# Moving the tiny per-token columns of two layer norms into an idle PSUM bank of a four-layer transformer kernel

## The chip, the cores and the metric

The kernel runs on one core of one Trainium2 chip. The metric is the device time of one execution in microseconds (us); lower is better. The engines are TensorE (PE in the profile), VectorE (DVE), ScalarE (ACT), GpSimd (POOL) and SyncE (SP, which here only issues DMAs). Each has its own instruction queue, works in order, and waits for the others through semaphores.

## What is computed

The input `x` has 2 x 512 tokens of 1024 features, the context has 2 x 1024 tokens. Four residual blocks follow each other, each behind a layer norm without weights:

```
x = x + tanh(g_xattn[0]) * fake_quant(LN(x)) @ fake_quant(ctx)
x = x + tanh(g_ffn[0])   * (quant_per_token(LN(x)) @ dequant(W_int).T + bias)
x = x + tanh(g_xattn[1]) * attention(LN(x), ctx, ctx; Wq, Wk, Wv, Wo)
x = x + tanh(g_ffn[1])   * (LN(x) @ dequant_fp4(packed).T)

LN(x)              = (x - mean(x)) / sqrt(var(x) + 1e-5)
quant_per_token(x) = clip(round(x / s), -127, 127) * s,  s = clip(max|x|, 1e-8) / 127
```

The change concerns the second norm (with the per-token quantisation behind it) and the third norm. Both need, for each token, a handful of single numbers: the mean, the variance, its inverse root, the quantisation step.

## The kernel before

The 1024 tokens lie on 128 partitions in T = 8 tiles `t`; `X[:, t, :]` (128 x 1024, fp32, in SBUF) is the residual stream of tile `t`. A per-token number of all tiles is a column block of 8: `mv[:, t, 0:2]` (mean, variance), `sd` (the square root that ScalarE makes), `rr` (inverse root), `ra` (a scratch), `am` (absolute maximum), `step_`, `ninv` (minus one over the step), `sB` (scale of the second product), `bb` (bias of the third norm), `nhalf`. All of them lie in SBUF, all in fp32.

The stages: up to about 150 us the context and the weights are prepared, the first norm is made and K and V are projected. Then comes the stage that the change touches, called the AB stage here (about 151 to 252 us): product "a" (first residual block) and product "b" (second) of the 8 tiles, in the order of the list `AB_OPS` (L165): a0 to a4, b0, a5, b1, a6, b2, a7, b3 to b7. TensorE's `stage_ab` (L1462) fills three pairs of PSUM banks in turn, banks (0,1), (4,5), (2,3) (`AB`, L164); it may begin operation i only when VectorE has emptied operation i - 3 (L1477). Banks 6 and 7 (`sbank` 2 and 3) are not used by it: their last use before it is the transposes of the integer weights (`wd_turn`, L1386, emptied by `wd_high` and `wd_low`), and bank 7's next use is the attention (`sum_half`, L1559).

VectorE's order in the AB stage is written out by hand in L1195 to L1229. For each tile it does

- `a_out(t)` (through `ab_out`, L1137): X = product * scale + X for the two halves, two SCALAR_TENSOR_TENSOR of 128x512 at L1146; then `a_stats(t)` (`stats`, L1003): mean and variance;
- `ln2_reduce(t)` (L1160): the maximum over |mean - x| that ScalarE has written (`ln2_deviation`, L767), then three tiny operations to the step and to `ninv`, for which ScalarE's `ln2_round` (L772) waits;
- `ln2_clip(t)` (L1170): the clip of the 16-bit quantised tile at L1172, after which SP transposes it by DMA for product b;
- `ln2_scales(p)` (L1174), once for tiles 0 to 3 and once for 4 to 7: the inverse root by `root_of` (L1010, one Newton step on the reciprocal of ScalarE's square root) and `sB`; `b_out` needs `sB`;
- `b_out(t)` (L1156): the same as `a_out` for product b with `sB` as scale, and the statistics of the third norm;
- `ln3_affine(p)` (L1180) for each pair of tiles: `root_of` again and `bb`; ScalarE's `y3_out` (L784) waits for it and makes the normalised tile and its 16-bit high part, GpSimd's `y3_low` (L515) the low part, and SP transposes both.

`d()` is an explicit drain, so each tiny operation starts after the one before it has written. The first norm's `ln1_affine` (L1050) uses `root_of` too and isn't touched.

GpSimd's order is also written by hand (L519 to L544): `wq_low(k)` (a TENSOR_SCALAR at L504 and a TENSOR_TENSOR at L506, 128x1024), `add_bias(t)` (TENSOR_TENSOR, L513), `add_c2(t)` (L493), `y3_low(t)` (L517). ScalarE has its own (L810 to L835): deviation, rounding, the square roots (`ln_sd`, L673), `wq_high(k)` (L797) and `y3_out(t)`. SP issues `xt2`, `next_wq`, `xt3` in L352 to L362, then the load `praw` of the packed weights (L365), the stores of q (`store_q`) with `xt3(6)` and `xt3(7)` between them (L394 to L397).

Behind the AB stage: the q projection (`q_proj`, from 245 us), with the unpacking of the last weights on VectorE (`unpack`, L1236, which begins only when all of `xt3` has landed, L1279), then from 325 us the score maxima, the attention and the last two products.

Of the kernel before, what the change touches and what calls it, by code (L numbers as in the profile page):

```python
# [21 lines left out]
ALU = mybir.AluOpType  # L22
AX = mybir.AxisListType
# [5 lines left out]
EPS = 1e-5  # L29
MAGIC = 12582912.0  # L30
ZC = 128.0
WS = 256.0
# [5 lines left out]
def build(nc, x, ctxt, g_xattn, g_ffn, x1s, x1z, x2s, x2z, W_int, scale_i32, bias, Wq, Wk, Wv, Wo,  # L38
# [4 lines left out]
    T = B * S // P  # L43
    TB = S // P
# [31 lines left out]
    with ExitStack() as ctx:  # L76
        def sb(name, shape, dt):
            return ctx.enter_context(nc.sbuf_tensor(name, shape, dt))

        def sem(name):  # L80
            return ctx.enter_context(nc.semaphore(name))
# [3 lines left out]
        bank = [mpair[0][:, 0, :], mpair[0][:, 1, :], mpair[1][:, 0, :], mpair[1][:, 1, :],  # L85
                sbank[0][:, :], sbank[1][:, :], sbank[2][:, :], sbank[3][:, :]]
# [23 lines left out]
        mv = sb("mv", [P, T, 2], F32)  # L110
        rs = sb("rs", [P, 8], F32)
        sd = sb("sd", [P, T], F32)
        nhalf = sb("nhalf", [P, T], F32)
        rr = sb("rr", [P, T], F32)
        bb = sb("bb", [P, T], F32)
        ra = sb("ra", [P, T], F32)
        sB = sb("sB", [P, T], F32)
        am = sb("am", [P, T], F32)
        step_ = sb("step", [P, T], F32)
        ninv = sb("ninv", [P, T], F32)  # L120
# [20 lines left out]
        at = [0, SET, 8192]  # L141
# [12 lines left out]
        dev = [cx[:, 2 + i, :] for i in range(2)]  # L154
# [10 lines left out]
        AB_OPS = ([("a", t) for t in range(5)] + [("b", 0), ("a", 5), ("b", 1), ("a", 6), ("b", 2), ("a", 7)]  # L165
                  + [("b", t) for t in range(3, T)])

        acc_sb = y[:, 0:512]
        rsum_sb = y[:, 512:1024]
        sumT_sb = vtmp[:, 0:512]  # L170
# [27 lines left out]
        s = {n: sem(n) for n in names}  # L198
# [721 lines left out]
        def _(dve):  # L920
            v = nc.vector

            def d():

                dve.drain()  # L925
# [9 lines left out]
            def consts():  # L935
                dve.wait_ge(s["gates_ok"], 1)
                v.reciprocal(IS1, S1)
                v.reciprocal(IS2, S2)
                v.tensor_tensor(AL, TX0, S1, ALU.mult)
                v.tensor_scalar(NZ1, Z1, -1.0, ZC, ALU.mult, ALU.add)  # L940
                v.tensor_scalar(NZ2, Z2, -1.0, ZC, ALU.mult, ALU.add)
                v.tensor_scalar(BE, TF0, 1.0 / WS, None, ALU.mult)
                v.tensor_scalar(GA, TX1, 1.0 / WS, None, ALU.mult)
                v.tensor_scalar(NBE, TF0, -1.0 / WS, None, ALU.mult)
                d()
                v.tensor_tensor(AL, AL, S2, ALU.mult)
                v.tensor_tensor(KZZ, NZ1, NZ2, ALU.mult)
                d()
                v.tensor_tensor(NZ1A, NZ1, AL, ALU.mult)
                v.tensor_tensor(NZ2A, NZ2, AL, ALU.mult)  # L950
                v.tensor_tensor(KZZ, KZZ, AL, ALU.mult)
                d()
                v.tensor_scalar(KZZ, KZZ, float(D), None, ALU.mult).then_inc(s["consts_ok"], 1)
# [56 lines left out]
            def root_of(first, n, ok, at):  # L1010

                c = slice(first, first + n)
                v.tensor_scalar(nhalf[:, c], mv[:, c, 1], EPS, -0.5, ALU.add, ALU.mult)
                dve.wait_ge(ok, at)
                v.reciprocal(rr[:, c], sd[:, c])
                d()
                v.tensor_tensor(ra[:, c], rr[:, c], rr[:, c], ALU.mult)
                d()
                v.tensor_tensor(ra[:, c], ra[:, c], nhalf[:, c], ALU.mult)
                d()  # L1020
                v.scalar_tensor_tensor(out=rr[:, c], in0=ra[:, c], scalar=1.5, in1=rr[:, c], op0=ALU.add, op1=ALU.mult)
                d()
# [46 lines left out]

            turned_low(0, 0)  # L1070
            consts()
            wkv_low(2)
            turned_low(1, 2)
# [46 lines left out]
            c = NCH - 1  # L1120
# [38 lines left out]

            def ln2_reduce(t):  # L1160
                dve.wait_ge(s["ln2_dev"], t + 1)
                v.tensor_reduce(am[:, t:t + 1], dev[t % 2], AX.X, ALU.max, apply_absolute_value=True)
                d()
                v.tensor_scalar(step_[:, t:t + 1], am[:, t:t + 1], 1e-8 * EPS ** 0.5, 1.0 / 127.0, ALU.max, ALU.mult)
                d()
                v.tensor_scalar(ra[:, t:t + 1], step_[:, t:t + 1], -1.0, None, ALU.mult)
                d()
                v.reciprocal(ninv[:, t:t + 1], ra[:, t:t + 1]).then_inc(s["ln2_inv"], 1)

            def ln2_clip(t):  # L1170
                dve.wait_ge(s["ln2_q"], t + 1)
# [1 line left out]

            def ln2_scales(p):  # L1174
                c = slice(TB * p, TB * p + TB)
                root_of(TB * p, TB, s["ln2_sd"], p + 1)
                v.scalar_tensor_tensor(out=sB[:, c], in0=step_[:, c], scalar=BE, in1=rr[:, c], op0=ALU.mult, op1=ALU.mult)
                d()

            def ln3_affine(p):  # L1180
                c = slice(2 * p, 2 * p + 2)
                d()
                root_of(2 * p, 2, s["ln3_sd"], p + 1)
                v.scalar_tensor_tensor(out=bb[:, c], in0=mv[:, c, 0], scalar=-1.0, in1=rr[:, c], op0=ALU.mult,
                                       op1=ALU.mult).then_inc(s["ln3_aff"], 1)

            def ln4(t, first=False):
# [8 lines left out]
            a_stats(0)  # L1196
            a_out(1)
            ln2_reduce(0)
            a_stats(1)
            for t in range(2, 5):  # L1200
                a_out(t)
                ln2_clip(t - 2)
                ln2_reduce(t - 1)
                a_stats(t)
                if t == 2:
                    bias_scale()
            ln2_scales(0)
            ln2_clip(3)
            ln2_reduce(4)
            for t in range(5, T):  # L1210
                b_out(t - 5)
                if t == 6:
                    ln3_affine(0)
                a_out(t)
                a_stats(t)
                ln2_clip(t - 1)
                ln2_reduce(t)
            ln2_scales(1)
            b_out(3)
            ln2_clip(7)  # L1220
            ln3_affine(1)
            b_out(4)
            b_out(5)
            ln3_affine(2)
            b_out(6)
            b_out(7)
# [463 lines left out]
```

## Time and profile before

| | us |
|---|---|
| median of 3 runs | 934.3 (928.06, 934.3, 934.41) |
| the profiled execution | 933.91 |
| its span | 932.1 |

| engine | busy, us | share of the span |
|---|---|---|
| PE | 848.9 | 91% |
| DVE | 598.2 | 64% |
| POOL | 534.8 | 57% |
| ACT | 447.6 | 48% |

The span is what the profiler sees from the first to the last instruction of that one execution; 1.8 us of the device time lie around it. The shares are averages over stages with different limits. In the rows below, times are in us from the start of the span, the second number of a timeline row is the time of the instruction (or of the merged group), and brackets give the idle time of the engine before it and what ended it. An instruction that is held up inside its engine shows as a long one, not as idle time before it.

### The profile page before, as it was taken

The numbers are of one execution on the slowest core, as the hardware profiler recorded it, in microseconds if no ns is written. First come the engines' busy times: TensorE is split into PE (matmuls) and PEld (weight loads), VectorE is DVE, ScalarE is ACT, GpSimd is POOL, SyncE is SP. The second block draws the span as 40 slices with busy tenths as digits, with TensorE's granted clock in tenths as the row PEclk, the third lists the DMA queues.
The fourth block names the chain that finished last, engine by engine and source line by source line (L and its number), as shares of the span: only waits on it lengthen the run. The fifth ranks groups of instructions, "written<-read, shape, count | busy, mean of one in ns | idle before, by whom it ended". The sixth has DMA issues, their size and how long they took to land.

```text
span 932.1 us, 14107 instructions
## 1 busy us (share of the span) xinstructions
PE 848.9 (91%) x4456; PEld 333.4 (36%) x4456; DVE 598.2 (64%) x846; ACT 447.6 (48%) x741; POOL 534.8 (57%) x235
## 2 busy tenths in 40 slices
PE   3789899969978797999999999999999998999998
PEld 2656564424433242222222222222222222444443
DVE  3666655988746645777777777877777850264621
ACT  4243425636511112667767767677767776022100
POOL 3544216964732310788888888888888888222100
PEclk9999999989989897999999999999999999999999
DMA  6898873422887421254455444544555334222232
GB/s 203 220 225 228 200 194 91 102 68 63 154 213 201 113 76 54 46 123 99 100 122 122 95 91 104 121 104 93 121 121 113 65 80 91 46 46 56 56 124 79
DMA packets 121673, 107.80 MB, mean 116 GB/s; under 512 B 86176, under 2 KB 106656, under 8 KB 117536
## 3 DMA queue, kind: packets, MB, share of 16 engines
q1 hardware_dynamic: 116160, 73.69, 31.0%
q0 software_dynamic: 4608, 33.56, 17.8%
q8 instruction: 26, 0.43, 0.2%
q10 hardware_dynamic: 864, 0.00, 0.0%
q14 instruction: 15, 0.12, 0.0%
HBM read 41.55 MB, written 12.58 MB: 58 GB/s over the span
## 4 chain that ended last, share of the span: by engine, by line
PE 57%; DVE 16%; issue 9%; DVEq 6%; DMA 6%; SPq 2%; ACT 2%; POOLq 2%; POOL 1%; ACTq 0%
PE sbank L1546 11%; PE sbank L1555 10%; PE mpair L1500 9%; DVEq L925 6%; DVE mx L1262 5%; PE sbank L1632 3%; PE sbank L1647 3%; PE sbank L1634 3%; PE sbank L1649 3%; PE sbank L1636 3%; PE sbank L1399 2%; PE sbank L1401 2%; PE sbank L1400 2%; PE sbank L1565 2%; POOLq L485 2%
## 5 line engine op out<-in xcount | busy, mean ns | idle before, releaser
L1262 DVE TENSOR_REDUCE mx<-mpair 128x1 f32<-128x1024 f32 x256 | 301.1, 1215 | 80.9 <-PE mpair L1500 80.7
L867 ACT ACTIVATE regC<-sbank 128x512 f32<-128x512 f32 x512 | 279.6, 595 | 130.7 <-PE sbank L1546 130.1
L1546 PE MATMUL sbank<-regD 98*128 98x512 f16 x512 | 179.8, 388 | 9.4 <-DMA regD<-mT 5.2
L1500 PE MATMUL mpair<-regD 96*128 96x512 f16 x512 | 158.1, 386 | 11.5 <-DVE mx L1262 6.4
L588 POOL TENSOR_TENSOR wraw<-regC 128x2048 f32<-128x2048 f32 x32 | 145.3, 4541 | 23.4 <-ACT regC L867 14.1
L1555 PE MATMUL sbank<-regC,regD 128*32 128x512 f32 x1024 | 137.2, 608 | 1.0 <-ACT regC L867 1.0
L1546 PEld LDWEIGHTS sbank<-regD 98*128 98x128 f16 x512 | 46.6, 97 | 202.1 <-ACT regC L867 162.3
L588 POOL TENSOR_TENSOR regD<-regC 128x2048 f32<-128x2048 f32 x16 | 72.8, 4552 | 54.2 <-ACT regC L867 54.2
L588 POOL TENSOR_TENSOR tail<-regC 128x2048 f32<-128x2048 f32 x16 | 76.7, 4796 | 0.6 <-ACT regC L867 0.6
L1500 PEld LDWEIGHTS mpair<-regD 96*128 96x128 f16 (+1 forms) x512 | 49.4, 99 | 64.4 <-DVE mT L1272 11.3
L484 POOL TENSOR_SCALAR xT_lo<-xT_lo,sc 128x1024 f32<-128x1024 f32 x16 | 29.9, 1868 | 65.2 <-DVE X L971 47.3
L1399 PE MATMUL sbank<-xT_hi,regC 128*128 128x512 f16 x128 | 51.1, 399 | 9.6 <-DVE tail L1233 8.6
L1400 PE MATMUL sbank<-xT_lo,regC 128*128 128x512 f16 x128 | 50.9, 398 | 0.0
L1401 PE MATMUL sbank<-xT_hi,regC 128*128 128x512 f16 x128 | 50.7, 396 | 0.0
L626 POOL TENSOR_TENSOR tail<-y,r 128x1024 f16<-128x1024 f32 x8 | 17.1, 2131 | 55.9 <-ACT r L908 55.9
L504 POOL TENSOR_SCALAR wraw<-wraw 128x1024 f32<-128x1024 f32 x16 | 17.5, 1097 | 54.4 <-ACT regR L808 34.7
L1632 PE MATMUL sbank<-regR,xT_hi 128*128 128x512 f16 x128 | 48.5, 379 | 0.0
L1647 PE MATMUL sbank<-regK,xT_hi 128*128 128x512 f16 x128 | 48.5, 379 | 0.0
L1634 PE MATMUL sbank<-regR,xT_hi 128*128 128x512 f16 x128 | 48.5, 379 | 0.0
L1636 PE MATMUL sbank<-regR,xT_lo 128*128 128x512 f16 x128 | 48.5, 379 | 0.0
L1649 PE MATMUL sbank<-regK,xT_lo 128*128 128x512 f16 x128 | 48.5, 379 | 0.0
L1006 DVE BATCH_NORM_STATS2 stt<-X 128x6 f32<-128x512 f32 (+1 forms) x64 | 40.8, 680 | 9.9 <-DMA X<-in_x 6.2
(170 smaller groups left out, 1267.7 us busy)
## 6 DMA issues: line engine op xcount, KB each, us to landing
regD<-wraw POOLq DMA_DIRECT2D x16, 1024.0 KB, 7.0
tail<-wraw POOLq DMA_DIRECT2D x16, 1024.0 KB, 7.0
xT_lo<-in_ctx SPq DMA_DIRECT2D x16, 512.0 KB, 5.2
wraw<-in_L_ffn_W_int SPq DMA_DIRECT2D x8, 512.0 KB, 4.7
X<-in_x SPq DMA_DIRECT2D x4, 1024.0 KB, 7.4
wraw<-in_L_xattn_Wq SPq DMA_DIRECT2D x8, 512.0 KB, 4.0
wraw<-in_L_xattn_Wo SPq DMA_DIRECT2D x8, 512.0 KB, 4.5
regD<-q_hi_scratch SPq DMA_DIRECT2D x32, 128.0 KB, 2.4
```

The costliest lines, as they stand in the source:

```text
L588: nc.gpsimd.tensor_tensor(p_sum[pr if pr < 3 else 1][:, :, :], probs[:, (2 * pr) % 4, :, :], probs[:, (2 * pr) % 4 + 1, :, :], ALU.add).th ...
L867: nc.scalar.activation(probs[:, kt % 4, h, :], bank[4 + h % 2], ACT.Exp, scale=SCALE).then_inc(s["exp_ok"], 1)
L1262: v.tensor_reduce(mx[m][:, bass.ds(n, 1)] if par is not None else mx[m][:, n:n + 1], slot[:, :, :], AX.XY, ALU.max).then_inc(s["mx_red"], 1)
L1399: pe.matmul(dst, whi(k), xhi(k), start=(k == 0), stop=False)
L1500: m = pe.matmul(mpair[slot][:, half, :], qst[par][0:96, bass.ds(n * P, P)], kst[par][0:96, half * 512:(half + 1) * 512], start=True, stop= ...
L1546: pe.matmul(bank[4 + h % 2], kst[par][0:98, kt * P:(kt + 1) * P], qst[par][0:98, h * 512:(h + 1) * 512], start=True, stop=True).then_inc(s ...
L1555: m = pe.matmul(bank[6][HD * h:HD * h + HD, :], vst[par][:, kt * HD:(kt + 1) * HD], probs[:, kt % 4, h, :], start=(kt == 0), stop=(kt == K ...
L1632: pe.matmul(bank[4 + h], xT_hi[:, k, bass.ts(t, P)], wo_hi[:, k, h * H2:(h + 1) * H2], start=(k == 0), stop=False)
L1634: pe.matmul(bank[4 + h], xT_hi[:, k, bass.ts(t, P)], wo_lo[:, k, h * H2:(h + 1) * H2], start=False, stop=False)
L1636: m = pe.matmul(bank[4 + h], xTl[:, k, bass.ts(t, P)], wo_hi[:, k, h * H2:(h + 1) * H2], start=False, stop=(k == KD - 1))
L1647: pe.matmul(bank[6 + h], xT_hi[:, k, bass.ts(t, P)], w2T[:, k, h * H2:(h + 1) * H2], start=(k == 0), stop=False)
L1649: m = pe.matmul(bank[6 + h], xTl[:, k, bass.ts(t, P)], w2T[:, k, h * H2:(h + 1) * H2], start=False, stop=(k == KD - 1))
```

## The change

A view of five column blocks of 8 in bank 7 is made: `ra_p`, `am_p`, `step_p`, `mr_p`, `rh_p`. `ln2_reduce` keeps its four operations, but the maximum, the step and its negative lie in PSUM. `root_of` is replaced, for the second and third norm, by `newton`: with `r` the reciprocal of the square root, it makes `ra_p = r * r` and `ra = (var + EPS) * ra_p`; the inverse root is then (ra - 3) * (-r / 2), and what multiplies it is folded in: `ln2_scales` gives `sB = (ra - 3) * (step * NBE * r)` with the constant `NBE` now -0.5 times the gate, and `ln3_affine` gives `rr = (ra - 3) * rh_p` and `bb = (ra - 3) * mr_p`. Operations: `ln2_reduce` 4 before and after; `ln2_scales` 6 before, 5 after; `ln3_affine` 6 before, 7 after.

```diff
+        ra_p, am_p, step_p, mr_p, rh_p = (bank[7][:, T * i:T * i + T] for i in range(5))
...
-                v.tensor_scalar(NBE, TF0, -1.0 / WS, None, ALU.mult)
+                v.tensor_scalar(NBE, TF0, -0.5 / WS, None, ALU.mult)
...
             def ln2_reduce(t):
                 dve.wait_ge(s["ln2_dev"], t + 1)
-                v.tensor_reduce(am[:, t:t + 1], dev[t % 2], AX.X, ALU.max, apply_absolute_value=True)
-                d()
-                v.tensor_scalar(step_[:, t:t + 1], am[:, t:t + 1], 1e-8 * EPS ** 0.5, 1.0 / 127.0, ALU.max, ALU.mult)
-                d()
-                v.tensor_scalar(ra[:, t:t + 1], step_[:, t:t + 1], -1.0, None, ALU.mult)
-                d()
-                v.reciprocal(ninv[:, t:t + 1], ra[:, t:t + 1]).then_inc(s["ln2_inv"], 1)
+                v.tensor_reduce(am_p[:, t:t + 1], dev[t % 2], AX.X, ALU.max, apply_absolute_value=True)
+                d()
+                v.tensor_scalar(step_p[:, t:t + 1], am_p[:, t:t + 1], 1e-8 * EPS ** 0.5, 1.0 / 127.0, ALU.max, ALU.mult)
+                d()
+                v.tensor_scalar(ra_p[:, t:t + 1], step_p[:, t:t + 1], -1.0, None, ALU.mult)
+                d()
+                v.reciprocal(ninv[:, t:t + 1], ra_p[:, t:t + 1]).then_inc(s["ln2_inv"], 1)
+
+            def newton(c, ok, at):
+
+                dve.wait_ge(ok, at)
+                v.reciprocal(rr[:, c], sd[:, c])
+                d()
+                v.tensor_tensor(ra_p[:, c], rr[:, c], rr[:, c], ALU.mult)
+                d()
+                v.scalar_tensor_tensor(out=ra[:, c], in0=mv[:, c, 1], scalar=EPS, in1=ra_p[:, c], op0=ALU.add,
+                                       op1=ALU.mult)
+                d()
...
             def ln2_scales(p):
                 c = slice(TB * p, TB * p + TB)
-                root_of(TB * p, TB, s["ln2_sd"], p + 1)
-                v.scalar_tensor_tensor(out=sB[:, c], in0=step_[:, c], scalar=BE, in1=rr[:, c], op0=ALU.mult, op1=ALU.mult)
+                newton(c, s["ln2_sd"], p + 1)
+                v.scalar_tensor_tensor(out=step_p[:, c], in0=step_p[:, c], scalar=NBE, in1=rr[:, c], op0=ALU.mult,
+                                       op1=ALU.mult)
+                d()
+                v.scalar_tensor_tensor(out=sB[:, c], in0=ra[:, c], scalar=-3.0, in1=step_p[:, c], op0=ALU.add,
+                                       op1=ALU.mult)
                 d()
 
             def ln3_affine(p):
                 c = slice(2 * p, 2 * p + 2)
                 d()
-                root_of(2 * p, 2, s["ln3_sd"], p + 1)
-                v.scalar_tensor_tensor(out=bb[:, c], in0=mv[:, c, 0], scalar=-1.0, in1=rr[:, c], op0=ALU.mult,
+                newton(c, s["ln3_sd"], p + 1)
+                v.scalar_tensor_tensor(out=mr_p[:, c], in0=mv[:, c, 0], scalar=0.5, in1=rr[:, c], op0=ALU.mult,
+                                       op1=ALU.mult)
+                v.tensor_scalar(rh_p[:, c], rr[:, c], -0.5, None, ALU.mult)
+                d()
+                v.scalar_tensor_tensor(out=rr[:, c], in0=ra[:, c], scalar=-3.0, in1=rh_p[:, c], op0=ALU.add,
+                                       op1=ALU.mult)
+                v.scalar_tensor_tensor(out=bb[:, c], in0=ra[:, c], scalar=-3.0, in1=mr_p[:, c], op0=ALU.add,
                                        op1=ALU.mult).then_inc(s["ln3_aff"], 1)
```

## Rows read from the trace of the kernel before

**Rows 1.** Page, part 4: the chain that ended last, by engine.
```profile
PE 57%; DVE 16%; issue 9%; DVEq 6%; DMA 6%; SPq 2%; ACT 2%; POOLq 2%; POOL 1%; ACTq 0%
```

**Rows 2.** Windows: PE, PEld, DVE, ACT, POOL busy, clock, DMA share, GB/s.
```profile
195.00:252.00 57.00, 56.01 (x254) 24.95 (x253) 49.32 (x100) 29.74 (x31) 31.90 (x18) 0.98 0.48 97
```

**Rows 3.** Timeline of VectorE, 182 to 192 us: `ln2_scales(0)` and the clip behind it.
```profile
182.52 2.33 DVE L1013 TENSOR_SCALAR nhalf<-mv 128x4 f32<-128x4 f32 x1
...
185.00 0.84 DVE L1017 TENSOR_TENSOR ra<-rr 128x4 f32<-128x4 f32 x1
...
186.16 1.96 DVE L1021 SCALAR_TENSOR_TENSOR rr<-ra,rr 128x4 f32<-128x4 f32 x1
188.19 2.22 DVE L1177 SCALAR_TENSOR_TENSOR sB<-step,sc,rr 128x4 f32<-128x4 f32 x1
190.49 1.20 DVE L1172 TENSOR_SCALAR tail<-tail 128x1024 f16<-128x1024 f16 x1
```

**Rows 4.** Timeline of GpSimd, 182 to 196 us.
```profile
182.45 2.37 POOL L513 TENSOR_TENSOR X<-X,tail 128x1024 f32<-128x1024 f32 x1
184.77 1.06 POOL L504 TENSOR_SCALAR wraw<-wraw 128x1024 f32<-128x1024 f32 x1
185.98 2.12 POOL L506 TENSOR_TENSOR regC<-wraw,regC 128x1024 f16<-128x1024 f32 x1
188.06 2.34 POOL L513 TENSOR_TENSOR X<-X,tail 128x1024 f32<-128x1024 f32 x1
190.36 1.05 POOL L504 TENSOR_SCALAR wraw<-wraw 128x1024 f32<-128x1024 f32 x1
...
193.64 2.36 POOL L513 TENSOR_TENSOR X<-X,tail 128x1024 f32<-128x1024 f32 x1
```

**Rows 5.** Lines of VectorE by source: a tiny, a PSUM-sourced and a wide form.
```profile
L1164 DVE TENSOR_SCALAR step<-am x8: 153/154/155, 160.6 to 223.0; 128x1 f32<-128x1 f32 x8
L1270 DVE TENSOR_SCALAR mT<-mpair x16: 278/279/280, 363.1 to 759.7; 16x128 f16<-16x128 f32 x16
L1146 DVE SCALAR_TENSOR_TENSOR X<-mpair,sB,X x12: 727/743/752, 193.4 to 246.9; 128x512 f32<-128x512 f32 x12
```

**Rows 6.** Timeline of TensorE: two pauses of the AB stage and behind it.
```profile
194.34 5.22 PE L1481 MATMUL mpair<-regR,xT_hi 128*128 128x512 f16 x16 [8.16 <-DVE X L1146]
...
245.45 0.38 PE L1399 MATMUL sbank<-xT_hi,regC 128*128 128x512 f16 x1 [0.99 <-DMA xT_lo<-regR]
```

**Rows 7.** Timeline of VectorE: a clip, then `root_of` of three later passes.
```profile
199.39 0.37 DVE L1172 TENSOR_SCALAR r<-r 128x1024 f16<-128x1024 f16 x1
...
205.71 1.66 DVE L1013 TENSOR_SCALAR nhalf<-mv 128x2 f32<-128x2 f32 x1
...
223.56 1.63 DVE L1013 TENSOR_SCALAR nhalf<-mv 128x4 f32<-128x4 f32 x1
...
237.16 0.87 DVE L1013 TENSOR_SCALAR nhalf<-mv 128x2 f32<-128x2 f32 x1
...
238.17 1.93 DVE L1017 TENSOR_TENSOR ra<-rr 128x2 f32<-128x2 f32 x1
240.18 0.93 DVE L1019 TENSOR_TENSOR ra<-ra,nhalf 128x2 f32<-128x2 f32 x1
...
241.43 1.96 DVE L1184 SCALAR_TENSOR_TENSOR bb<-mv,rr 128x2 f32<-128x2 f32 x1
```

**Rows 8.** Timeline of GpSimd beside those passes.
```profile
204.98 2.35 POOL L513 TENSOR_TENSOR X<-X,tail 128x1024 f32<-128x1024 f32 x1
...
235.64 2.36 POOL L513 TENSOR_TENSOR X<-X,tail 128x1024 f32<-128x1024 f32 x1
237.96 2.13 POOL L517 TENSOR_TENSOR regR<-y,regR 128x1024 f16<-128x1024 f32 x1
```

**Rows 9.** Chain in order of time (start, us, what) behind the AB stage.
```profile
251.33 1.24 ACT vtmp L790
...
268.61 0.43 DVE regR L1238
```

## The prediction

> **What bounds the kernel now.** I read the page's chain first: TensorE carries 57% of it, VectorE 16% [rows 1]. A change to tiny VectorE work can pay only in the stages where VectorE is on that chain, so the next view was the chain in order of time: between 159 and 251 us it is nearly all VectorE (maxima, statistics, the two-half evictions, the roots), and it goes on from there over ScalarE's third norm at 251.33 to the unpacking at 268.61 [rows 9]. In the window 195 to 252 VectorE is busy 49.3 of 57 us, and TensorE 56.0 [rows 2]: the two are close, which limits what a faster VectorE can bring.
>
> The timeline of VectorE then shows what is odd. A 128x1 operation takes 0.154 us [rows 5], but in `ln2_scales(0)` operations on four columns take 2.33, 0.84, 1.96 and 2.22 us [rows 3]. Beside GpSimd's timeline each of them ends with a GpSimd instruction: 182.52 + 2.33 = 184.85 and the add of 182.45 ends at 184.82; 185.84 and 185.83; 188.12 and 188.10; 190.41 and 190.40 [rows 3, 4]. So these are waits for a wide GpSimd instruction to finish. All four read two SBUF tensors, or are a TENSOR_SCALAR from SBUF to SBUF over an even number of columns. What isn't held: the one-column TENSOR_SCALAR (maximum 155 ns of 8), and L1146, which reads one tensor from PSUM and one from SBUF: 727 to 752 ns in all of 12, GpSimd busy or not [rows 5]. The same is seen at 205.71 (ends with GpSimd's 207.33), 223.56, and four times from 237.16 (0.87, 1.93, 0.93, 1.96) [rows 7, 8].
>
> The Trainium skill (SBUF — State Buffer, Who interferes with whom) says the same of reads: an operation with two SBUF inputs contends with a GpSimd instruction that reads SBUF, one with at most one SBUF input outside the two-port modes doesn't. What it adds speaks against part of the change: by it the destination doesn't free `rr * rr`, whose inputs both stay in SBUF, nor `mr_p`. I cost both as held, as their nearest rows of the trace are.
>
> **The change, part by part.** A tiny operation with its drain takes 0.24 us (0.16 busy, 0.08 until the next starts: 186.16 to 188.19 less the hold; I use it throughout).
>
> *`ln2_scales(0)` and the clip behind it.* Before: 182.52 to 190.41, then the clip L1172 waits until 191.69 [rows 3]. After: `nhalf` is gone, the reciprocal runs at once, `rr * rr` starts at 182.76 and is held to 184.85 by the add of 182.45 [rows 4]. Its nearest row is L1017, the same operation with another destination, 0.84 and 1.93 us when held [rows 3, 7]. Then three operations with a PSUM source, free: 184.92 to 185.65. The clip starts at 185.7 and is held by L504 to 185.83; a held clip ends 0.28 behind GpSimd (191.69 against 191.41, the end of the L504 of 190.36) [rows 3, 4], so 186.11. Gain 191.69 - 186.11 = 5.6 us. If a PSUM destination did free `rr * rr`, the end would be about 1.0 us earlier.
>
> *What takes some back.* Everything behind moves 5.6 us earlier and meets GpSimd elsewhere, since GpSimd runs back to back on work that doesn't depend on VectorE until 196.0. The next clip moves from 199.39, where it took 0.37, to 193.8 and now meets the add of 193.64 to 196.00 [rows 4, 7]: it ends at 196.28, not 194.2. Of this 2.1 us loss about 1.1 remain (the maximum of tile 5 had waited 0.93 for ScalarE). The next add, L513 of 204.98 to 207.33 before, moves only as ScalarE's `wq_high(5)` allows and then ends at about 201.7. In `ln3_affine(0)`, before 205.71 to 208.39, the statistics end at 201.2, the reciprocal waits for ScalarE's root (0.3 us; `nhalf` used to lie beside it), and from 201.75 nothing is held: end 202.9. Cumulated gain 5.5 us.
>
> *`ln2_scales(1)`.* Before, `nhalf` is held 1.63 us and the rest takes 1.1. After, `rr * rr` is held to the same GpSimd end, and 0.8 us follow. Cumulated 5.8.
>
> *`ln3_affine(1)` and (3)*: the first wasn't held. One operation less held, one more issued, 0.3 us for the root: within 0.2 us of nothing each. *`ln3_affine(2)`*, before 237.16 to 243.39, 6.2 us [rows 7]. After, in the same frame: `rr * rr` is held to 238.0 by the add of 235.64, `ra` is free, `mr_p` at 238.4 has two SBUF inputs and is held to 240.1 by L517 of 237.96 [rows 8], then `rh_p` (PSUM destination; taken as free, if held 1.0 more) and the last two: end 240.7. Gain 2.7, cumulated 8.5.
>
> *`ln2_reduce`, 8 times.* Three operations get a PSUM source. Price: L1270 reads 128 columns of PSUM in 0.279 us and L1146 512 in 0.743, 1.21 ns a column, which leaves 0.124 for no columns, no more than the 0.154 of the one-column SBUF form [rows 5]. I take 0. No row shows VectorE writing PSUM; the nearest are these two, so the bounds are 0.124 - 0.154 = -0.03 below and, if all that L1270 takes more than L1164 were PSUM's, 0.279 - 0.154 = 0.125 above. I take 0, nearest to the first, since a column has to cost something. For tiles 0 to 3 even that is hidden: they come before 182.5, and `rr * rr` is held to 184.85 whenever it arrives before. Some 45 operations on PSUM remain behind that, of which some 25 aren't under a hold: at most 3.1 us.
>
> A page would make it dearer: the Trainium skill (VectorE: DVE Perf Modes, The TRN2 errata) gives a PSUM source 62 cycles more than an SBUF source, 0.065 us; over the 30 operations with one that would be 2.0 us and a time near 927.5. L1270 doesn't show it.
>
> *TensorE as the next limit.* Its 8.16 us pause at 186 to 194 [rows 6] shrinks to about 2.7, and operation a6 may not run at the low clock (5.22 us for 16 matmuls is 0.33 each, the window's mean is 56.0 / 254 = 0.22 [rows 2, 6]). From b3 on it runs without a pause, now from 203.9, and five b blocks of 32 matmuls at 0.216, the mean without that slow start, 6.9 us each, end at 238.4. VectorE wants the last one at 237.7 and gets its second half at 238.6. So gains beyond 8.5 to 9.5 are cut off here. The q projection starts when the third norm of tile 3 has landed, before at 245.45 [rows 6], after at about 239.6, and is not late for ScalarE.
>
> *Behind the stage.* ScalarE's step of 251.33 moves to about 242.9. SP's transposes, the load of the packed weights and the first q store stand in the same order behind it, all 8 to 9 us earlier, so the unpacking of 268.61 [rows 9] starts at 260.2. From there on nothing is tied to an absolute time. Sum: 933.9 - 8.4 = 925.5 us, for the profiled execution; its 933.91 is 0.4 below the median of 934.3. I forecast 926.0, 0.9% less, giving back half a microsecond for PSUM.
>
> **The rivals.** *A, the held operations that remain cost more*: `rr * rr`, `mr_p` and the moved clips meet a GpSimd instruction each time. For it: of 30 operations that can be held (5 in each of six passes) 10 remain, six `rr * rr` and four `mr_p`, and a hold is up to 2.3 us. Against it: tiles wait for the same GpSimd ends anyway. Two more holds of 2 us that stay: gain 4.4, 929.5.
>
> *B, the PSUM destination frees them too*, and TensorE's clock stays up across the shorter pause. Then VectorE is 10 us or more ahead, TensorE's five blocks cut it at about 9.5, and the q projection at full clock gives 2 more: 922.5.
>
> *C, slower*: tiny writes to PSUM are slow to become readable, and each drain waits for them. Place: the 48 operations of `ln2_reduce` (tiles 4 to 7: 16), `ln2_scales` (8) and `ln3_affine` (24) that touch PSUM. It decides from 8.4 / 48 = 0.175 us each, a doubling; at 0.4 each it costs 19, and the time is 945. Against it: L1270 followed by L1272 shows no sign on the read side.
>
> *D, the gain is hidden anyway*: the chain behind 251 us waits for DMA, and the load of the packed weights meets other transfers. The load is issued only behind the transposes, so it moves along. If it didn't, only some 2 us would stay: 932.
>
> **How the numbers follow.** Forecast 45%, A 25%, B 17%, D 9%, C 4%. A measurement of this kernel can tell about 1% from no change, that is 9.3 us; the runs before are 6.3 us apart. Forecast with its own uncertainty of 2 us: faster by over 1% in a third of it; B all but always; A and D within 1%. Faster 0.33, same 0.64, slower 0.03. The range reaches from B, with 1 us for its spread, to A and part of D: 921.5 to 931.
>
> **What would show it.** Right: `ln2_scales(0)` 3.1 us long in place of 7.9 with one long operation, `rr * rr`, ending with a GpSimd instruction; all PSUM-sourced tiny operations at 0.15 to 0.23; TensorE's pause of 8.16 near 3; the clip of tile 4 about 2.4 us; in `ln3_affine(2)` two holds in place of four; the unpacking's first row near 260. Wrong: `rr * rr` short beside a busy GpSimd (B), tiny PSUM operations above 0.25 or gaps above 0.1 between them (C), more holds than I counted (A), or the unpacking's start near 266 (D).

## The result, and the profile after

The changed kernel takes 923.4 us in the median of 5 runs (920.4 to 923.85), the kernel before 933.73 (5 runs): ratio 0.9889, 95% interval 0.9862 to 0.9916. The forecast was 926.0, range 921.5 to 931. Timed once more later (experiment 5) the same kernel gave 925.18 and a ratio of 0.9925 (0.9902 to 0.9948). The profiled execution took 923.4 us, its span is 921.6 against 932.1: 10.5 us less.

The chain that ended last, by engine, page part 4 of the changed kernel:

```profile
PE 60%; DVE 13%; DMA 7%; issue 7%; SPq 5%; DVEq 4%; ACT 1%; POOLq 1%; POOL 0%; ACTq 0%
```

VectorE has 13% of the chain in place of 16%, and its drains 4% in place of 6% [rows 1]. Where they went is in the timelines. VectorE from the first `ln2_scales` on, changed kernel (start, us, line, operation, tiles; `sbank` is the PSUM bank), and the clips of tiles 3 and 4 behind it:

```profile
180.98 0.12 DVE L1174 RECIPROCAL rr<-sd 128x4 f32<-128x4 f32 x1
181.18 2.08 DVE L1176 TENSOR_TENSOR sbank<-rr 128x4 f32<-128x4 f32 x1
183.34 0.16 DVE L1178 SCALAR_TENSOR_TENSOR ra<-mv,sbank 128x4 f32<-128x4 f32 x1
183.58 0.23 DVE L1189 SCALAR_TENSOR_TENSOR sbank<-sbank,sc,rr 128x4 f32<-128x4 f32 x1
183.89 0.16 DVE L1192 SCALAR_TENSOR_TENSOR sB<-ra,sbank 128x4 f32<-128x4 f32 x1
184.12 0.43 DVE L1184 TENSOR_SCALAR tail<-tail 128x1024 f16<-128x1024 f16 x1
...
192.67 2.07 DVE L1184 TENSOR_SCALAR r<-r 128x1024 f16<-128x1024 f16 x1
```

GpSimd's timeline beside them:

```profile
180.88 2.36 POOL L514 TENSOR_TENSOR X<-X,tail 128x1024 f32<-128x1024 f32 x1
183.21 1.04 POOL L505 TENSOR_SCALAR wraw<-wraw 128x1024 f32<-128x1024 f32 x1
184.39 2.14 POOL L507 TENSOR_TENSOR regC<-wraw,regC 128x1024 f16<-128x1024 f32 x1
...
192.09 2.36 POOL L514 TENSOR_TENSOR X<-X,tail 128x1024 f32<-128x1024 f32 x1
```

One tiny operation is long, `rr * rr`: it ends at 183.26, GpSimd's add at 183.24. The three behind it read PSUM and take 0.16 to 0.23 us while GpSimd's L505 runs. From the start of the first operation to the last one's end it is 3.07 us; before it was 7.89 [rows 3]. The clip of tile 4, which took 0.37 us [rows 7], now runs into the add of 192.09 and takes 2.07.

The third norm of tiles 4 and 5, VectorE and then GpSimd, against the passes from 237.16 in [rows 7, 8]:

```profile
230.47 0.40 DVE L1176 TENSOR_TENSOR sbank<-rr 128x2 f32<-128x2 f32 x1
230.95 0.16 DVE L1178 SCALAR_TENSOR_TENSOR ra<-mv,sbank 128x2 f32<-128x2 f32 x1
231.19 1.76 DVE L1200 SCALAR_TENSOR_TENSOR sbank<-mv,rr 128x2 f32<-128x2 f32 x1
232.86 0.15 DVE L1202 TENSOR_SCALAR sbank<-rr 128x2 f32<-128x2 f32 x1
```
```profile
228.49 2.36 POOL L514 TENSOR_TENSOR X<-X,tail 128x1024 f32<-128x1024 f32 x1
230.80 2.12 POOL L518 TENSOR_TENSOR regR<-y,regR 128x1024 f16<-128x1024 f32 x1
```

The two operations with two SBUF inputs end at 230.87 and 232.95, the two GpSimd instructions at 230.85 and 232.92. Two holds are left of four.

What tiny operations cost with PSUM, the source view of L1165 (duration in ns, minimum, median, maximum):

```profile
L1165 DVE TENSOR_SCALAR sbank<-sbank x8: 166/166/168, 159.0 to 216.1; 128x1 f32<-128x1 f32 x8
```

166 ns against 154 [rows 5]. TensorE's pause and VectorE's wait for the last product block, each from its engine's timeline:

```profile
187.25 5.30 PE L1503 MATMUL mpair<-regR,xT_hi 128*128 128x512 f16 x16 [2.72 <-DVE X L1147]
```
```profile
236.57 0.73 DVE L1147 SCALAR_TENSOR_TENSOR X<-mpair,sB,X 128x512 f32<-128x512 f32 x1
237.48 0.75 DVE L1147 SCALAR_TENSOR_TENSOR X<-mpair,sB,X 128x512 f32<-128x512 f32 x1 [0.18 <-PE mpair L1507]
```

The pause is 2.72 us in place of 8.16 [rows 6], and at the stage's end VectorE has just begun to wait for TensorE. The chain behind the stage, for [rows 9]:

```profile
241.55 1.24 ACT vtmp L791
...
258.89 0.43 DVE regR L1260
```

To see which part of the 10.5 us belongs to the change, the stage has to be measured from its own start. In the table "start" is VectorE's first eviction of the AB stage (153.38 before, 151.74 after), and each landmark counts from there.

| from the start, us | before | after | difference |
|---|---|---|---|
| end of the clip behind the first `ln2_scales` | 38.31 | 32.81 | -5.50 |
| end of `ln3_affine(0)` | 55.01 | 49.75 | -5.26 |
| end of the second `ln2_scales` | 72.90 | 67.31 | -5.59 |
| end of `ln3_affine(2)` | 90.01 | 81.57 | -8.44 |
| ScalarE's third norm of tile 6 | 97.95 | 89.81 | -8.14 |
| first unpacking | 115.23 | 107.15 | -8.08 |

The rest of the 10.5 us is 1.64 before the stage begins and 0.8 between the unpacking and the end (663.5 us before, 662.7 after). Outside the AB stage the two kernels have the same instructions, but for the value of one constant. The time from the unpacking to the end lies between 661.1 and 666.1 us in the twelve executions of this document whose work there is the same, so the 0.8 is within its scatter.

### The profile page after: what moved, and what is told of

It is laid out like the page before. It is cut to its first block, busy times and chain, and to the rows that moved or that the text cites. A ratio compares the mean times of both kernels' runs of the same rounds, so it can differ in the third digit from the quotient of the medians.

```text
span 921.6 us, 14109 instructions
## 1 busy us (share of the span) xinstructions
PE 846.8 (92%) x4456; PEld 333.4 (36%) x4456; DVE 590.9 (64%) x848; ACT 448.4 (49%) x741; POOL 534.1 (58%) x235
## 4 chain that ended last, share of the span: by engine, by line
PE 60%; DVE 13%; DMA 7%; issue 7%; SPq 5%; DVEq 4%; ACT 1%; POOLq 1%; POOL 0%; ACTq 0%
PE sbank L1568 11%; PE sbank L1577 10%; PE mpair L1522 9%; DVE mx L1284 5%; DVEq L926 4%; PE sbank L1654 3%; PE sbank L1669 3%; PE sbank L1671 3%; PE sbank L1656 3%; PE sbank L1658 3%; PE sbank L1587 2%; PE mpair L1506 2%; PE mpair L1507 2%; PE sbank L1422 2%; PE sbank L1421 2%
## 5 line engine op out<-in xcount | busy, mean ns | idle before, releaser
L1421 PE MATMUL sbank<-xT_hi,regC 128*128 128x512 f16 x128 | 49.9, 390 | 9.2 <-DVE tail L1255 8.8
L1423 PE MATMUL sbank<-xT_hi,regC 128*128 128x512 f16 x128 | 49.7, 388 | 0.0
L505 POOL TENSOR_SCALAR wraw<-wraw 128x1024 f32<-128x1024 f32 x16 | 17.2, 1077 | 51.7 <-ACT regR L809 37.4
```

## The experiments

"The stage" is always the time from the first eviction of the AB stage to ScalarE's third norm of tile 6: 97.95 us before, 89.81 after. Ratios are against runs of the kernel before on the same chip. The expectations in microseconds count from its first 933.9 us; beside experiments 1 to 4 it measured 931.23 (19 runs), beside 5 to 8 932.39 (11 runs). The medians of experiments 1 and 4 therefore lie 0.5 and 1.3 us under their expected ranges, while their distances to the kernel before fit.

**1. The new formula with its columns in SBUF.**

```diff
-        ra_p, am_p, step_p, mr_p, rh_p = (bank[7][:, T * i:T * i + T] for i in range(5))
+        tiny = sb("tiny", [P, 5 * T], F32)
+        ra_p, am_p, step_p, mr_p, rh_p = (tiny[:, T * i:T * i + T] for i in range(5))
```

> The changed kernel with its five column blocks in SBUF instead of PSUM; formula, order and number of operations as in the changed kernel. Theory H (a VectorE operation with two SBUF inputs, or an even TENSOR_SCALAR from SBUF to SBUF, waits for the running GpSimd instruction; a PSUM input frees it): 4 operations of ln2_scales and 6 of ln3_affine can be held again; the first ln2_scales with its clip ends about 1 us earlier than in the kernel before at best, the pass beside GpSimd at 237 us is as long as before; 931 to 935 us in all. Rival F (the gain is the new formula, whose operations are fewer on the path, wherever its columns lie): as the changed kernel, 923 to 924.

Measured: 930.5 us, ratio 0.9996 (0.9979 to 1.0013), stage 97.37. VectorE in the first `ln2_scales`, and GpSimd:

```profile
181.68 0.93 DVE L1177 TENSOR_TENSOR tiny<-rr 128x4 f32<-128x4 f32 x1
182.70 0.92 DVE L1179 SCALAR_TENSOR_TENSOR ra<-mv,tiny 128x4 f32<-128x4 f32 x1
183.69 0.22 DVE L1190 SCALAR_TENSOR_TENSOR tiny<-tiny,sc,rr 128x4 f32<-128x4 f32 x1
183.99 1.93 DVE L1193 SCALAR_TENSOR_TENSOR sB<-ra,tiny 128x4 f32<-128x4 f32 x1
```
```profile
180.24 2.36 POOL L515 TENSOR_TENSOR X<-X,tail 128x1024 f32<-128x1024 f32 x1
182.56 1.04 POOL L506 TENSOR_SCALAR wraw<-wraw 128x1024 f32<-128x1024 f32 x1
183.75 2.15 POOL L508 TENSOR_TENSOR regC<-wraw,regC 128x1024 f16<-128x1024 f32 x1
```

The same operations are held once their inputs lie in SBUF: the ends 182.61, 183.62 and 185.92 are GpSimd's 182.60, 183.60 and 185.90. The one at 183.69 slipped into the gap between two GpSimd instructions. The formula alone shortens the stage by 0.6 us and is worth nothing that the total time shows; F has fallen.

**2. The old formula with am, step and ra in PSUM.**

```diff
-            def root_of(first, n, ok, at):
+            def root_of(first, n, ok, at, ra=ra):
...
-                root_of(TB * p, TB, s["ln2_sd"], p + 1)
-                v.scalar_tensor_tensor(out=sB[:, c], in0=step_[:, c], scalar=BE, in1=rr[:, c], op0=ALU.mult, op1=ALU.mult)
+                root_of(TB * p, TB, s["ln2_sd"], p + 1, ra_p)
+                v.scalar_tensor_tensor(out=sB[:, c], in0=step_p[:, c], scalar=BE, in1=rr[:, c], op0=ALU.mult, op1=ALU.mult)
...
-                root_of(2 * p, 2, s["ln3_sd"], p + 1)
+                root_of(2 * p, 2, s["ln3_sd"], p + 1, ra_p)
```

(`ln2_reduce` is as in the changed kernel.)

> The kernel before with its old formula, but am, step and ra of the second and third norm in PSUM (nhalf, rr, mv stay in SBUF). Theory H: nhalf, rr*rr and bb can still be held, two of the five operations of ln2_scales; the first ln2_scales with its clip ends 3.4 us earlier than before relative to the stage's start (5.6 in the changed kernel), the pass at 237 us 2.3 us shorter (2.7); 926 to 929 us. Rival F: as the kernel before, 933 to 934. Rival P (all of the gain is placement): as the changed kernel, 923 to 924.

Measured: 927.29 us, ratio 0.9957 (0.9940 to 0.9973), stage 92.49, that is 5.5 us of the 8.1. The clip behind the first `ln2_scales` ends 3.25 us earlier (expected 3.4), and from the end of `ln3_affine(1)` to that of `ln3_affine(2)` it is 10.04 us against 12.31 before and 9.40 after, 2.3 less as expected. Placement gives two thirds and the new formula the rest. The two kernels differ in `nhalf`, whose input `mv` and output stay in SBUF here, and in `bb`, which has no PSUM input here. In the first `ln2_scales` of this trace `nhalf` is held until 182.88, so that `rr * rr` meets the next GpSimd instruction and is held again until 183.89: two holds where the changed kernel has one. How the rest divides between `nhalf` and `bb` was not tried. P has fallen too: it is the two together.

**3. A second reciprocal into PSUM, so that no tiny operation has two SBUF inputs.**

```diff
+                v.reciprocal(rr_p[:, c], sd[:, c])
                 d()
-                v.tensor_tensor(ra_p[:, c], rr[:, c], rr[:, c], ALU.mult)
+                v.tensor_tensor(ra_p[:, c], rr[:, c], rr_p[:, c], ALU.mult)
...
-                v.scalar_tensor_tensor(out=mr_p[:, c], in0=mv[:, c, 0], scalar=0.5, in1=rr[:, c], op0=ALU.mult,
+                v.scalar_tensor_tensor(out=mr_p[:, c], in0=mv[:, c, 0], scalar=0.5, in1=rr_p[:, c], op0=ALU.mult,
```

> The changed kernel plus a second reciprocal that writes the inverse root into PSUM too; rr*rr and mr_p then have one PSUM input each, so that no tiny operation of the two norms has two SBUF inputs. Theory H: none is held, each at 0.15 to 0.23 us; the first ln2_scales gains 1.0 us more (its clip is then held by the same GpSimd add), the stage 1.5 to 3 us before TensorE's blocks cut it off: 921 to 922.5 us. Rival (a PSUM destination or the doubled reciprocal costs what the hold did): 923 to 924.

Measured: 921.14 us, ratio 0.9883 (0.9866 to 0.9901), stage 87.13. The changed kernel was not timed beside it, and its first ratio, 0.9889, is no different; so experiment 6 times the two side by side.

**4. Only `ln2_reduce` in PSUM.** The kernel before with the four operations of `ln2_reduce` as in the changed kernel, and

```diff
-                v.scalar_tensor_tensor(out=sB[:, c], in0=step_[:, c], scalar=BE, in1=rr[:, c], op0=ALU.mult, op1=ALU.mult)
+                v.scalar_tensor_tensor(out=sB[:, c], in0=step_p[:, c], scalar=BE, in1=rr[:, c], op0=ALU.mult, op1=ALU.mult)
```

> The kernel before with only ln2_reduce's maximum, step and negative in PSUM (and sB made from that step). Theory H: nothing held in ln2_reduce before, so 0.05 us is lost in each of 8 passes; sB is no longer held, 2 us in the first ln2_scales, of which the clip behind it gives back half: 932 to 933.5 us. Rival C (PSUM is dear for tiny operations): slower than before, above 935.

Measured: 930.68 us over 10 runs, ratio 0.9995 (0.9977 to 1.0014), stage 97.06. The last rows of the first `ln2_scales` and its clip:

```profile
186.41 1.96 DVE L1022 SCALAR_TENSOR_TENSOR rr<-ra,rr 128x4 f32<-128x4 f32 x1
188.44 0.22 DVE L1178 SCALAR_TENSOR_TENSOR sB<-sbank,sc,rr 128x4 f32<-128x4 f32 x1
188.74 2.19 DVE L1173 TENSOR_SCALAR tail<-tail 128x1024 f16<-128x1024 f16 x1
```

`sB` takes 0.22 us where it took 2.22 [rows 3], and the clip, 1.20 there, now takes 2.19: half of the freed hold is handed to the next operation that can be held. C (PSUM is dear) has fallen: the stage is not longer but 0.9 us shorter.

**5. The changed kernel once more.** No edit.

> The changed kernel unaltered, once more. The time from the first eviction of the AB stage to the third norm of tile 6 should be 89.8 us again (98.0 in the kernel before), while the time to that first eviction may be anywhere between 151 and 154 us. If the 1.6 us that it was earlier in the changed kernel's profile belong to the change, it is 151.7 again here and the ratio to the kernel before is 0.989; if they are the start's own scatter, the ratio is about 0.991.

Measured: 925.18 us, ratio 0.9925 (0.9902 to 0.9948), stage 89.83, first eviction at 152.23. The stage repeats to 0.02 us. The start, 0.49 us later than in the first run, lies between the two cases of the expectation; the interval of the ratio holds 0.991 and not 0.989. Experiments 9 to 11 follow the start up.

**6. The kernel of experiment 3 beside the changed kernel.**

> The kernel with the second reciprocal once more, beside the changed kernel on the same chip. Theory H with TensorE as the next limit: AB stage to tile 6 in 87.1 us, VectorE waits some 2.5 us for the last product block, and the median is 1 to 2.7 us under the changed kernel's. Rival (the second reciprocal brings nothing): the same median within 0.3 us.

Measured: 921.74 us against 925.18 for the changed kernel timed beside it, ratio to before 0.9888 (0.9864 to 0.9913), stage 87.16. First `ln2_scales`, GpSimd beside it, and VectorE at the last product block:

```profile
183.43 0.17 DVE L1177 TENSOR_TENSOR sbank<-rr,sbank 128x4 f32<-128x4 f32 x1
183.68 0.16 DVE L1179 SCALAR_TENSOR_TENSOR ra<-mv,sbank 128x4 f32<-128x4 f32 x1
183.91 0.23 DVE L1190 SCALAR_TENSOR_TENSOR sbank<-sbank,sc,rr 128x4 f32<-128x4 f32 x1
184.22 0.16 DVE L1193 SCALAR_TENSOR_TENSOR sB<-ra,sbank 128x4 f32<-128x4 f32 x1
184.46 1.24 DVE L1185 TENSOR_SCALAR tail<-tail 128x1024 f16<-128x1024 f16 x1
...
236.95 0.75 DVE L1147 SCALAR_TENSOR_TENSOR X<-mpair,sB,X 128x512 f32<-128x512 f32 x1 [2.53 <-PE mpair L1508]
```
```profile
183.05 2.36 POOL L514 TENSOR_TENSOR X<-X,tail 128x1024 f32<-128x1024 f32 x1
185.38 1.23 POOL L505 TENSOR_SCALAR wraw<-wraw 128x1024 f32<-128x1024 f32 x1
```

All four tiny operations run under the add of 183.05 to 185.41 without a hold, `rr * rr` in 0.17 us in place of 2.08. Only the wide clips are held (this one, and that of tile 4 with 1.33 us). And VectorE waits 2.53 us for TensorE where it waited 0.18: of the time won on VectorE, that much is cut off by the five blocks in a row. Timed side by side this version beats both kernels: against the changed one the stage is 2.7 us shorter and the median 3.4. Experiment 11 shows that the 2.7 are not there in each execution.

**7. The kernel before beside a GpSimd with little to do.** Most of the bias and of the low part of Wq is left out.

```diff
-                nc.gpsimd.tensor_tensor(X[:, t, :], X[:, t, :], biasB, ALU.add).then_inc(s["bias_add"], 1)
+                nc.gpsimd.tensor_tensor(X[:, t, 0:2], X[:, t, 0:2], biasB[:, 0:2], ALU.add).then_inc(s["bias_add"], 1)
...
-                split_lo(k, wq_hi, wq_lo, s["wq_hi_ok"], s["wq_ok"])
...
+                nc.gpsimd.tensor_scalar(wraw[:, k % 2, 0:2], wraw[:, k % 2, 0:2], WS, 1.0, ALU.mult, ALU.mult)
...
+                nc.gpsimd.tensor_tensor(wq_lo[:, k, 0:2], wraw[:, k % 2, 0:2], wq_hi[:, k, 0:2],
+                                        ALU.subtract).then_inc(s["wq_ok"], 1)
```

> The kernel before, its VectorE work untouched, but GpSimd's bias adds and its part of splitting Wq act on 2 of 1024 columns: nearly all of the bias and of the low part of Wq is left out. Theory H: with no wide GpSimd instruction beside them the SBUF-only tiny operations of ln2_scales and of ln3_affine at 205, 223 us take 0.16 to 0.23 us in their old form, and the clips behind tile 3 take 0.4; only y3_low at 237 us still holds some; the stage is 9 to 12 us shorter, 919 to 925 us. Rival S (these operations are slow of themselves, or by ScalarE or DMA traffic): they stay at 0.8 to 2.3 us, and the time at 930 or above.

Measured: 915.17 us, ratio 0.9825 (0.9791 to 0.9858), stage 85.01. VectorE's untouched operations:

```profile
180.43 0.12 DVE L1017 TENSOR_SCALAR nhalf<-mv 128x4 f32<-128x4 f32 x1
...
180.70 0.16 DVE L1021 TENSOR_TENSOR ra<-rr 128x4 f32<-128x4 f32 x1
180.94 0.16 DVE L1023 TENSOR_TENSOR ra<-ra,nhalf 128x4 f32<-128x4 f32 x1
181.18 0.17 DVE L1025 SCALAR_TENSOR_TENSOR rr<-ra,rr 128x4 f32<-128x4 f32 x1
181.42 0.22 DVE L1181 SCALAR_TENSOR_TENSOR sB<-step,sc,rr 128x4 f32<-128x4 f32 x1
181.72 0.43 DVE L1176 TENSOR_SCALAR tail<-tail 128x1024 f16<-128x1024 f16 x1
```

2.33, 0.84, 1.96 and 2.22 us [rows 3] have become 0.12, 0.16, 0.17 and 0.22 with not one VectorE instruction changed. S has fallen: it is GpSimd's wide instructions that made them long. As expected, one hold is left beside an instruction that stayed wide: in the pass at 225 us `nhalf` takes 0.80 us and ends at 226.22, GpSimd's `y3_low` at 226.20. The time is 4 us under the expected range. The stage gave 12.9 us where 9 to 12 were expected, of which 1.7 before the first `ln2_scales`, where the clips of tiles 0 and 2 are free too (0.43 us each; that of tile 1 is still held, 1.22, by an `add_c2`). Another 6.6 us lie behind the stage (2.2 up to the unpacking, 4.4 from there to the end). Part of the 4.4 is the scatter of that stretch: its 659.1 us are 2.0 under the shortest of the other twelve executions. Where the rest comes from was not settled.

**8. `rh_p` issued before `mr_p`.**

```diff
+                v.tensor_scalar(rh_p[:, c], rr[:, c], -0.5, None, ALU.mult)
                 v.scalar_tensor_tensor(out=mr_p[:, c], in0=mv[:, c, 0], scalar=0.5, in1=rr[:, c], op0=ALU.mult,
                                        op1=ALU.mult)
-                v.tensor_scalar(rh_p[:, c], rr[:, c], -0.5, None, ALU.mult)
```

> The changed kernel with rh_p (TENSOR_SCALAR, 2 columns, SBUF to PSUM) issued before mr_p, so that in the pass near 231 us it comes while GpSimd's y3_low runs. If a PSUM destination frees an even TENSOR_SCALAR, it takes 0.16 us there and mr_p behind it is held; if not, it takes 1.7 us and mr_p meets the next GpSimd instruction, up to 1 us more. The total stays within 1 us of the changed kernel's.

Measured: 924.21 us in one run, stage 89.83. VectorE, and GpSimd beside it:

```profile
232.15 0.16 DVE L1200 TENSOR_SCALAR sbank<-rr 128x2 f32<-128x2 f32 x1
232.22 1.70 DVE L1201 SCALAR_TENSOR_TENSOR sbank<-mv,rr 128x2 f32<-128x2 f32 x1
```
```profile
231.76 2.12 POOL L518 TENSOR_TENSOR regR<-y,regR 128x1024 f16<-128x1024 f32 x1
```

Under the same GpSimd instruction the two-column TENSOR_SCALAR from SBUF to PSUM takes 0.16 us and the operation with two SBUF inputs and a PSUM destination 1.70. The first is free and the second held, though both write PSUM. Experiment 6 has the free one too, 0.16 us at 200.94 and at 230.32 beside GpSimd instructions that run from 200.24 and 229.68. The held TENSOR_SCALAR of the kernel before, `nhalf`, differs from the free one in its destination and also in reading every second column of `mv`; no run changes the destination alone beside a running GpSimd instruction.

**9 to 11. Three kernels unaltered, for their start.** The kernel before, the changed kernel, and the kernel of the second reciprocal, one run each.

> The kernel before, unaltered, for its start. If the time to the first eviction of the AB stage belongs to the program (how its code lies, say), it is 153.4 us within 0.3; if it is scatter, anywhere from 151 to 154.

> The changed kernel, unaltered, for its start. Program: 151.7 to 152.2 us to the first eviction of the AB stage. Scatter: anywhere from 151 to 154. The stage itself 89.8 us in either case.

> The kernel of the second reciprocal, unaltered, for its start. Program: 153.7 to 153.9 us to the first eviction of the AB stage. Scatter: anywhere from 151 to 154. The stage 87.1 us in either case, with the block behind TensorE's pause of 1.7 us at 3.6 us for 16 matmuls and not at 5.3.

| kernel | first eviction at | stage | time |
|---|---|---|---|
| before | 153.38, 152.04 | 97.95, 97.97 | 933.91, 930.53 |
| changed (the first, 5, 10) | 151.74, 152.23, 150.76 | 89.81, 89.83, 89.58 | 923.4, 923.33, 921.04 |
| second reciprocal (3, 6, 11) | 153.65, 153.92, 153.26 | 87.13, 87.16, 89.86 | 923.55, 921.82, 924.27 |

(The times are those of the profiled executions.) Within one program the start moves by 0.7 to 1.5 us, so the 1.64 of the first comparison are about what scatter gives. The means of the rows also differ, by up to 2 us, with the same instructions up to there; three executions don't tell whether a part of that belongs to the program, and it stays open.

The third row has a surprise: the last stage is 89.86 and not 87.1. In its trace VectorE's scaling of the bias, 0.88 us in experiment 6, is held too, because GpSimd's instruction began 0.05 us before it and not 0.28 us after it. The timeline of TensorE shows what that leads to. VectorE and GpSimd, experiments 11 and 6:

```profile
169.00 2.36 POOL L494 TENSOR_TENSOR X<-X,xT_lo 128x1024 f32<-128x1024 f32 x1
169.05 2.87 DVE L1135 TENSOR_SCALAR tail<-tail,sc 128x1024 f32<-128x1024 f32 x1
...
238.99 0.75 DVE L1147 SCALAR_TENSOR_TENSOR X<-mpair,sB,X 128x512 f32<-128x512 f32 x1 [2.63 <-PE mpair L1508]
```
```profile
169.38 0.88 DVE L1135 TENSOR_SCALAR tail<-tail,sc 128x1024 f32<-128x1024 f32 x1
169.66 2.82 POOL L494 TENSOR_TENSOR X<-X,xT_lo 128x1024 f32<-128x1024 f32 x1
```

TensorE's operation a6 in experiments 11 and 6:

```profile
188.76 5.30 PE L1504 MATMUL mpair<-regR,xT_hi 128*128 128x512 f16 x16 [2.37 <-DVE X L1147]
```
```profile
188.39 3.61 PE L1504 MATMUL mpair<-regR,xT_hi 128*128 128x512 f16 x16 [1.67 <-DVE X L1147]
```

Counted from the first eviction, the clip behind the first `ln2_scales` ends at 32.81 us in experiment 11, as in the changed kernel, and at 31.78 in experiment 6; a6 starts at 35.50 and at 34.47, and it takes 5.30 us in place of 3.61. Together that is 2.72 us, all of the 2.70 by which the stage is longer, and it counts in full because TensorE is the limit in this kernel: VectorE waits 2.5 to 2.6 us for it in either case. In the changed kernel, where VectorE is the limit, the same 1.7 us of TensorE (experiment 10: 3.61 at a pause of 2.40; the first run: 5.30 at 2.72) move the stage by 0.25. The hold itself is not peculiar to this kernel: the same operation takes 2.86 to 2.87 us in experiments 5, 9 and 10 and 0.88 to 0.89 in the first runs of both kernels, and there the stage is the same with it (89.83, 97.97, 89.58) as without it (89.81, 97.95), for later operations wait for the same GpSimd ends.

## Why the prediction was right

It said 0.9% and 8.4 us, all of it in the AB stage; the stage gave 8.1 in two executions and 8.4 in a third.

- *The holds.* That the long tiny operations wait for GpSimd was read from their ends [rows 3, 4]; experiment 7 shows it by taking GpSimd away, experiment 1 by giving the inputs back to SBUF.
- *The first `ln2_scales` and clip*: predicted 5.6, measured 5.50; its length 3.1 and 3.07. `rr * rr` was costed as held though it writes PSUM, and is held (2.08 us). That was the step most in doubt, and the half of rival B that rested on it has fallen. The clip behind it was expected to be held until a GpSimd end and to end at 186.11, 32.73 us from the stage's start; it ended at 32.81.
- *What is taken back*: the clip of tile 4 was put at about 2.4 us and measured 2.07. `ln3_affine(0)`: 5.5 predicted, 5.26 measured. The 0.3 us for the wait on ScalarE's root is there, 0.36 in three passes.
- *Second `ln2_scales`*: 5.8 predicted, 5.59 measured. *`ln3_affine(2)`*: 8.5 and 8.44, with the two holds foreseen. `rh_p` as free: shown by experiment 8.
- *PSUM's own price* was taken as 0 and is 0.012 us for an operation (166 against 154 ns), 0.05 for a whole `ln2_reduce`. Four of eight passes lie where it counts, so 0.2 us. This is not the difference between 8.4 and 8.1: all of these passes lie before the end of `ln3_affine(2)`, where the count still stands at 8.44. The 0.3 us are lost behind it, where VectorE now idles 0.27 us before the eviction of 233.58 and 0.18 for TensorE's last block, against one hold less; in experiment 10, without the wait at the last block, the stage gave 8.4. The Trainium skill (VectorE: DVE Perf Modes, The TRN2 errata) would have made it 0.065; the measurement decides.
- *TensorE as the next limit*: the pause was put at 2.7 and is 2.72, and VectorE's wait at the last block has just begun (0.18). The second half came at 239.1 in the time of the kernel before (237.48 + 1.64), where 238.6 was forecast. The 0.216 us of a matmul in that sum is not the mean that the rows named there give, which is 0.213, but it is the distance between the matmuls in TensorE's timeline. Experiment 6 shows the limit itself, 2.53 us of waiting. Whether a6 escapes the low clock was left open; it does in one of three executions of the changed kernel (3.61 us), in the others its 16 matmuls take 5.30 as before (5.22 [rows 6]).
- *Rival A* (more holds stay): besides those costed, one of 0.27 us in `ln3_affine(0)` (`rr * rr`, 0.43), and no more. Of the ten operations that could still be held, five were: `rr * rr` four times and `mr_p` once. *Rival D*: the unpacking moved by 8.08, so the gain was not hidden; its absolute time was 258.9 and not 260.2 only through the earlier start. *Rival C*: fallen with experiment 4.
- *The level*: 926.0 was forecast and 923.4 measured. The 1.64 us of the start and 0.8 of the tail, in which nothing was changed, are in no step of the sum; the repeat gave 925.18. The two comparisons put the gain at 1.1% and 0.75% for a forecast of 0.9%. What its working got right is the 8.4 us of the stage. That the medians lie so near 926.0 is in part luck: within one kernel the start moves by up to 1.5 us and the stretch behind the unpacking by up to 1.7.

## What to carry to other kernels

A tiny VectorE operation that shows 1 to 2 us in a profile and ends together with a wide GpSimd instruction isn't slow but held; what frees it here is one input in PSUM, or, for an even-columned TENSOR_SCALAR with one SBUF input, a PSUM destination (experiments 6 and 8), and an idle bank with room for a few columns is enough. Give every one of them its PSUM input (here an extra reciprocal for 0.08 us), for each hold left, and each wide clip behind, takes part of the gain back. Look which engine is next before counting on more. To measure a change of this size, count from a landmark inside the kernel: the stage of the changed kernel repeated to 0.25 us, while its start moved by 1.5. Even then take more than one execution: the stage of the kernel with the second reciprocal, where TensorE is the limit, came out at 87.1 twice and at 89.9 once.

## What was not expected of the hardware

The holding goes both ways. In experiment 6 the clip, held by the add that ends at 185.41, runs from there to 185.70, and GpSimd's L505 of 185.38 takes 1.23 us in place of 1.04 in the changed kernel's trace at 183.21: GpSimd waits out the clip. The same line takes 1.22 us at 179.00 in the kernel before, behind a held clip that ends at 179.31, against 1.05 or 1.06 elsewhere in the stage. Which of the two waits is decided by who begins first: in experiment 6 the scaling of the bias begins at 169.38 and takes its 0.88 us, and GpSimd's L494 of 169.66 takes 2.82; in experiment 11 L494 begins first and takes 2.36, and the scaling 2.87. And a hold needs GpSimd to be inside an instruction: an operation that falls into the 0.15 us between two of them passes at once (experiment 1, 183.69), and the changed kernel's clip of 184.12, begun 0.13 us before L505 ends, takes 0.43 where a free one takes 0.37. So shifts of a tenth decide over a wait of two, yet later operations wait for the same GpSimd end and level it out again, as long as VectorE is the limit.

TensorE's clock. The windows over a6 in the first run of the changed kernel and in experiment 3 (window, its length, then busy time of PE, PEld, DVE, ACT and POOL, granted clock, DMA share, GB/s):

```profile
187.30:192.50 5.20, 5.20 (x17) 2.03 (x18) 4.54 (x8) 1.54 (x2) 5.05 (x4) 0.67 0.34 101
```
```profile
188.20:191.60 3.40, 3.40 (x17) 1.52 (x16) 3.21 (x6) 1.49 (x2) 3.40 (x3) 1.00 0.49 154
```

The granted clock is 0.67 on average after a pause of 2.72 us, and 1.00 after one of 1.66. The 0.67 is a part at 2.4 GHz and a part at 1.2: 0.95 from 187.30 to 188.60, so the clock is still high when the matmuls start, and 0.50 from 188.60 to 190.60. Between the two, pauses of 2.37 and 2.41 gave 5.30 us and one of 2.40 gave 3.61, so the length of the pause alone doesn't decide it.
